# Eight images side by side in the partitions: 16 KB rows in place of 4 KB rows in every DMA of a normalisation kernel

## What is computed

```python
def _gn(v, G=32, eps=1e-5):                      # 32 groups of 2 channels, per image
    g = v.reshape(B, G, C // G, H, W)
    m, s = mean(g), var(g)                       # over a group of one image
    return (g - m) / sqrt(s + eps)

def _L0_conv_ref(x):                             # masked batch norm
    m = x.sum(axis=1) != 0                       # the sum over all 64 channels
    ...                                          # mean and variance per channel, over batch and mask
    inv = 1.0 / sqrt(var + EPS)
    return where(m, x * inv, x)                  # and a rule for position (0, 0)

out = x + _L0_conv_ref(_gn(x))
```

## Time and profile before

| | |
|---|---|
| median of the runs | 1295.09 us |
| span of the profiled execution | 1293.2 us |
| HBM read + written | 268.44 + 268.44 MB, 415 GB/s over the span |
| DMA packets | 135469 |
| ScalarE busy | 816.4 us (63%) |
| VectorE busy | 796.5 us (62%) |
| TensorE busy | 741.7 us (57%) |
| GpSimd busy | 535.1 us (41%) |

### The profile page before, as it was taken

The page is one execution under the profiler, slowest core; times in us unless marked ns, Lnnn a source line. Parts: engine busy times, 40 slices in busy tenths (PEclk is TensorE's granted clock), DMA queues, the critical chain, the costliest instruction groups (busy, mean ns, idle before and its releaser), DMA issues.

```text
span 1293.2 us, 10692 instructions
## 1 busy us (share of the span) xinstructions
PE 741.7 (57%) x2882; PEld 302.4 (23%) x2882; DVE 796.5 (62%) x1892; ACT 816.4 (63%) x950; POOL 535.1 (41%) x504
## 2 busy tenths in 40 slices
PE   0766654566545665456654566544665446654475
PEld 0222222222222222122221222212222122222232
DVE  6776666566665666655666556665566655666563
ACT  0777555775557755567655676556765567755575
POOL 0055333454334544345443444434443444533450
PEclk9988767887678876688766887667887678866788
DMA  9999999999999999999999999999999999999997
GB/s 378 415 421 420 421 421 421 422 420 420 421 421 421 420 421 421 421 421 420 421 421 421 421 421 420 421 420 421 421 421 421 420 420 421 418 421 418 420 414 281
DMA packets 135469, 537.58 MB, mean 416 GB/s; under 512 B 4336, under 2 KB 4336, under 8 KB 135408
## 3 DMA queue, kind: packets, MB, share of 16 engines
q1 hardware_dynamic: 69936, 276.83, 52.3%
q10 hardware_dynamic: 65472, 260.05, 49.0%
HBM read 268.44 MB, written 268.44 MB: 415 GB/s over the span
## 4 chain that ended last, share of the span: by engine, by line
DMA 60%; ACT 15%; PE 11%; DVE 7%; issue 5%; SPq 0%; ACTq 0%
DMA out_dram<-slots 37%; DMA slots<-in_x_dram 23%; ACT slots L346 11%; PE flush L421 6%; ACT fresh L343 4%; DVE stats L471 2%; DVE spread L454 2%; PE stay L417 1%; PE stay L418 1%; PE small_ps L386 1%; PE small_ps L396 1%; DVE dev L517 1%; PE small_ps L397 1%; ACT sums L343 0%; SPq L237 0%
## 5 line engine op out<-in xcount | busy, mean ns | idle before, releaser
L471 DVE BATCH_NORM_STATS2 stats<-slots 128x6 f32<-128x512 f32 x1024 | 631.5, 680 | 437.8 <-DMA slots<-in_x_dram 436.5
L346 ACT ACTIVATE slots<-slots,out_bias,out_scale 128x1024 f32<-128x1024 f32 x512 | 622.4, 1245 | 2.3 <-DVE out_bias L528 1.3
L325 POOL TENSOR_TENSOR sums<-fresh,sums 128x512 f32<-128x512 f32 x360 | 458.8, 1274 | 363.6 <-ACT fresh L343 363.6
L421 PE MATMUL flush<-slots,weights 128*64 128x512 f32 x1536 | 442.0, 695 | 42.2 <-ACT fresh L343 40.6
L343 ACT ACTIVATE fresh<-flush,group_bias 128x512 f32<-128x512 f32 x360 | 246.5, 685 | 51.8 <-PE flush L421 51.8
L302 POOL TENSOR_TENSOR weights<-pair_sum,group_rstd 128x256 f32<-128x256 f32 (+1 forms) x128 | 73.2, 602 | 357.5 <-DVE group_bias L508 357.5
L421 PEld LDWEIGHTS flush<-slots,weights 128*64 128x64 f32 x1536 | 131.7, 156 | 295.9 <-issue 294.3
L358 ACT ACTIVATE by_image<-by_image,eps 128x16 f32<-128x16 f32 x32 | 9.8, 307 | 242.2 <-DVE by_image L495 241.8
L417 PE MATMUL stay<-slots,weights 128*64 128x512 f32 x512 | 140.0, 606 | 0.0
L418 PE MATMUL stay<-minus_mean,weights 128*64 128x512 f32 x512 | 138.1, 593 | 0.0
L386 PE MATMUL small_ps<-spread,group_avg 128*128 128x64 f32 x64 | 21.8, 443 | 183.3 <-DVE spread L491 183.3
(11 more groups left out here) (52 smaller groups left out, 234.5 us busy)
## 6 DMA issues: line engine op xcount, KB each, us to landing
slots<-in_x_dram SPq DMA_DIRECT2D x127, 2048.0 KB, 17.7
out_dram<-slots ACTq DMA_DIRECT2D x124, 2048.0 KB, 29.9
out_dram<-slots SPq DMA_DIRECT2D x16, 512.0 KB, 5.1
slots<-in_x_dram SPq DMA_DIRECT2D x4, 512.0 KB, 13.6
```

Of the source, the lines that this page charges most:

```text
L325: pool.tensor_tensor(into, fresh[:, n % FRESH_BUFS, :], into, ALU.add).then_inc(added, 1)
L346: nc.scalar.activation(out_in_ring(u, i), image_in_ring(u, i), ACT.Identity, bias=out_bias[:, u % 2, i:i + 1], scale=out_scale[:, u % 2, i ...
L421: nc.tensor.matmul(into, weight, source, start=True, stop=True).then_inc(image_summed, 1)
L471: last = V.bn_stats(stats[:, u % 2, k * BLOCK_STATS:(k + 1) * BLOCK_STATS], source)
```

## The change

In place of 128 rows of 4 KB of one image, a DMA now takes 16 rows of eight images (`SIDE` = 8). The 512 KB of a unit and image are cut into 16 rows of 32 KB (`SET_N` = 8192 elements), and partition `8 r + a` holds row `r` of image `a` of a set of eight; there are `SETS` = 2 sets per unit. A tile is the first or the second 16 KB of these 128 rows: 2 MB as before, in 128 contiguous pieces of 16 KB, both in DRAM and in a partition. The outermost dimension of the DRAM side of a DMA is now the 16 rows, the next the eight images. The last tile's loads and the last unit's stores take 1024 columns at a time (`chunk_in_dram`), as before 512 KB in 4 KB pieces.

The sums follow. A chunk of 1024 columns now holds a sixteenth of eight images instead of one image; all small operands have 2 columns where they had 16, with 32 values where there were 4 (`FOLDS`). `group_avg` is no longer one value: VectorE builds it from the unit matrix with two more instructions at the start, so that only the partitions of the same image are averaged, and the tenth load and all of TensorE wait for four matrices instead of two. `weights` has one matrix per set and sign instead of one per image. Number and width of the `bn_stats`, of the large matmuls, of ScalarE's large instructions and of GpSimd's additions are the same. The diff, cut to this (what it changes of the general path is left out):

```diff
-TILE_IMAGES = 4
+SIDE = 8
+TILE_CHUNKS = 4
...
-    FOLDS = 2 * BLOCKS
+    SETS = B // SIDE
+    SET_N = SIDE * N
+    SET_TILES = SET_N // TILE_N
+    FOLDS = 2 * BLOCKS * SIDE
...
-    x_rows, out_rows = (t.rearrange("b c w h -> b (c w h)").rearrange("b (u p n) -> u p b n", u=UNITS, p=P) for t in (x, out))
+    x_rows, out_rows = (t.rearrange("b c w h -> b (c w h)").rearrange("(t a) (u r n) -> u t r a n", a=SIDE, u=UNITS, n=SET_N)
+                        for t in (x, out))
...
-        weights = sb("weights", [P, 2, B, ROWS])
+        weights = sb("weights", [P, 2, 2, SETS, ROWS])
...
-        CONSTS, MATRICES = 8, 2
+        CONSTS, MATRICES = 8, 4
...
         def in_dram(rows, j):
-            i = j % UNIT_TILES * TILE_IMAGES
-            return rows[j // UNIT_TILES, :, i:i + TILE_IMAGES, :]
+            t, part = divmod(j % UNIT_TILES, SET_TILES)
+            return rows[j // UNIT_TILES, t, :, :, part * TILE_N:(part + 1) * TILE_N]
+
+        def chunk_in_dram(rows, u, i):
+            at = i % SIDE * N
+            return rows[u, set_of(i), :, :, at:at + N]
...
-                    sp.dma_start(in_ring(j), in_dram(x_rows, j)).then_inc(loaded[j % RING], 16)
+                    sp.dma_start(tile_in_ring(j), in_dram(x_rows, j)).then_inc(loaded[j % RING], 16)
...
-            def weigh(u, first, n, matrix):
-                at = u * B + first
-                return pool.tensor_tensor(weights[:, u % 2, first:first + n, :], matrix.unsqueeze(1).to_broadcast([P, n, ROWS]),
-                                          group_rstd[:, at:at + n].unsqueeze(2).to_broadcast([P, n, ROWS]), ALU.mult)
+            def weigh(u, t, sign, matrix):
+                at = u * SETS + t
+                return pool.tensor_tensor(weights[:, u % 2, sign, t, :], matrix,
+                                          group_rstd[:, at:at + 1].to_broadcast([P, ROWS]), ALU.mult)
...
-                act.dma_start(in_dram(out_rows, j), in_ring(j)).then_inc(stored[j % RING], 16)
+                act.dma_start(in_dram(out_rows, j), tile_in_ring(j)).then_inc(stored[j % RING], 16)
...
             V.tensor_scalar(minus_pair_sum[:, :], pair_sum[:, :], -1.0, None, ALU.mult).then_inc(matrices_ready, 1)
+            V.tensor_reduce(side[:, :], unit_matrix.rearrange("p (j a) -> p a j", a=SIDE), AX_X, ALU.add).then_inc(matrices_ready, 1)
+            dve.wait_ge(matrices_ready, 3)
+            V.tensor_scalar(group_avg[:, :].rearrange("p (j a) -> p j a", a=SIDE), side[:, :].unsqueeze(1).to_broadcast([P, P // SIDE, SIDE]),
+                            1.0 / (HALF_UNIT * IMAGE_FOLDS), None, ALU.mult).then_inc(matrices_ready, 1)
```

More of the change, by code:

```diff
@@ L71, in flush_order, with set_of, set_order @@
         return [i for i in sum_order(u) if i in flushed]
-    x_rows, out_rows = (t.rearrange("b c w h -> b (c w h)").rearrange("b (u p n) -> u p b n", u=UNITS, p=P) for t in (x, out))
+    x_rows, out_rows = (t.rearrange("b c w h -> b (c w h)").rearrange("(t a) (u r n) -> u t r a n", a=SIDE, u=UNITS, n=SET_N)
+                        for t in (x, out))
+    def set_of(i):
+        return i // SIDE
+    def set_order(u):
+        return sorted(range(SETS), key=lambda t: sum_order(u).index(next(i for i in sum_order(u) if set_of(i) == t)))
     ctx = ExitStack()
@@ L110, in norm_conv_kernel @@
         eps = sb("eps", [P, 2])
+        side = sb("side", [P, SIDE])
+        all_avg = sb("all_avg", [P, P])
         group_avg = sb("group_avg", [P, P])
@@ L143, in norm_conv_kernel @@
         small_ps = psum("small_ps", [P, BLK])
-        mean_ps, var_ps = (small_ps[:, i * B * FOLDS:(i + 1) * B * FOLDS] for i in range(2))
+        mean_ps, var_ps = (small_ps[:, i * SETS * FOLDS:(i + 1) * SETS * FOLDS] for i in range(2))
         bn_mean_ps, bn_var_ps, count_ps = (small_ps[:, 128 + i:129 + i] for i in range(3))
@@ L166, in norm_conv_kernel @@
         flag_ready = sem("flag_ready")
-        last_loaded = [sem(f"last_loaded{i}") for i in range(TILE_IMAGES)]
+        last_loaded = [sem(f"last_loaded{i}") for i in range(TILE_CHUNKS)]
         last_stored = sem("last_stored")
@@ L255, in _, with set_in_dram, set_on_chip, load_half @@
                         sp.dma_start(into[:, :, k, :], not_zero[k * ROWS:(k + 1) * ROWS, :, :]).then_inc(mask_spread, 16)
[L257 to L261, removed]
+                def set_in_dram(rows, u, t):
+                    return rows[bass.ds(u, 1), t, :, :, :].rearrange("o r a n -> (o r) a n")
+                def set_on_chip(v, t):
+                    at = t % HALF_SETS * SET_N
+                    return v[:, at:at + SET_N]
+                def load_half(u, a):
+                    for t in range(a * HALF_SETS, (a + 1) * HALF_SETS):
+                        sp.dma_start(set_on_chip(tile_x, t), set_in_dram(x_rows, u, t)).then_inc(tile_loaded, 16)
                 for sweep in range(2):
@@ L369, in _ @@
                     put_out(u, i)
-                    if u < LAST and i and i % TILE_IMAGES == 0:
-                        store(u, i // TILE_IMAGES - 1)
+                    if u < LAST and i and i % TILE_CHUNKS == 0:
+                        store(u, i // TILE_CHUNKS - 1)
                 if u < LAST:
@@ L413, in channel_sums @@
                     for k in range(BLOCKS):
-                        into, weight = bank[k * ROWS:(k + 1) * ROWS, :], weights[:, u % 2, i, :]
+                        into = bank[k * ROWS:(k + 1) * ROWS, :]
+                        weight = weights[:, u % 2, 1 if u == LAST and i in flushed else 0, t, :]
                         source = image_in_ring(u, i)[:, k * BLK:(k + 1) * BLK]
@@ L595, in tile_g @@
                 def tile_g(sweep, u, a, k):
-                    dve.wait_ge(tile_loaded, u * (HALVES * 16) + (sweep * GENERAL_TILES + a + 1) * 16)
-                    for i in range(HALF_IMAGES):
-                        at = bass.ds(u * B + (a * HALF_IMAGES + i), 1)
-                        last = V.tensor_scalar(tile_a[:, i * N:(i + 1) * N], tile_x[:, i * N:(i + 1) * N], group_mean[:, at],
+                    dve.wait_ge(tile_loaded, u * (HALVES * HALF_MOVES) + (sweep * GENERAL_TILES + a + 1) * HALF_MOVES)
+                    for i in range(HALF_SETS):
+                        at = bass.ds(u * SETS + (a * HALF_SETS + i), 1)
+                        columns = slice(i * SET_N, (i + 1) * SET_N)
+                        last = V.tensor_scalar(tile_a[:, columns], tile_x[:, columns], group_mean[:, at],
                                                group_rstd[:, at], ALU.subtract, ALU.mult)
```

144 lines of the change are left out of this document (80 added, 64 removed).

## The result

The changed kernel takes 1460.3 us (median of four runs, 1446.9 to 1469.9) where the kernel before takes 1295.1. The run of 1469.9 us counts as a slow one, and the ratio of the other three to the kernel before is 1.124, with an interval of 1.118 to 1.130. The forecast was 1270, so the sign was wrong; rival A is what happened, at a little over half of its price (165 us for 287). The runs of the changed kernel spread over 23 us, where those of the kernel before lie within 0.4 us; no run looked for the reason of this spread.

The account below looks back on a forecast made before the run. The DMA engines were taken to bound the kernel up to the last load's landing. Terms of -24.4, -0.2 and -0.3 us (-24.9) took 1295.1 to 1270.2 us; the range was 1255 to 1610, rivals included.

Parts of the forecast that it names:

- rival A: DMA engines moving eight neighbouring partitions each share a way into on-chip memory: 1.25 x DMA time, 1582 us, chance 0.38.
- What bounds the kernel: Up to the last load's landing at 1250.06 us, time is bytes over DMA rate; behind it DMA engines aren't full.
- Part 1: Loads and stores in 16 KB instead of 4 KB pieces: 1.95% less time up to the last landing, 24.4 us.
- The prediction's own sign for it: Sign of a wrong forecast: two directions cost more with 16 KB packets than with 4 KB ones.
- Its sign at the start: For shared ways on chip: tiles landing every 6 us or more already at the start, with loads alone.
- Parts 2 to 4: Small operands with fewer columns (0.2 us gained), fewer GpSimd weight instructions (0.3 us), two more instructions at the start (nothing).
- The end: Statistics, ScalarE's work and the rest behind the last load's landing: still 43 us after the change.
- Rivals B and C: B: images 16.8 MB apart slow DRAM, 1670 us, chance 0.06. C: packet time is all bytes, 1294.6 us, chance 0.10.

Follow-up runs that it names:

- streams: Kernel of DMAs only, thirty tiles loaded and thirty others stored, neither waiting for the other; all in 16 KB pieces: 337.6 us with eight images, 295.5 with four.

## Why the prediction was wrong

**What bounds the kernel: right.** The DMA engines are full before and after. Two readings were loose: the rate has fallen to 369 GB/s already at 1255 to 1262, and of the 43 us behind the last load, where the DMA engines were said not to be full, the stretch from 1270 to 1280 has a share of 1.02 at 403 GB/s.

**Part 1, its size: right where the split is right.** A unit went from 40.2 to 39.4 us with four images, for the forecast 39.5. Loads alone and mixed are both at 430 GB/s with 16 KB pieces, for 410 and 421 in the kernel before and 402 and 419 with four images in 4 KB pieces. At the same split a 16 KB packet saves 2.3% of a unit (40.28 to 39.37), and 2.6% of the rate in streams (431 against 420 GB/s). The forecast 1.95% was near, but partly by luck: it is three quarters of the gap between loads alone and loads with stores. That gap is gone with 16 KB pieces, but no run shows that it is what a packet costs as such.

**The step that failed: part 1, worked out as if the split over the DMA engines stayed the same.** Part 1 was to take 24.4 us off the time up to the last load's landing. That time went up by 157.3 us, from 1250.06 to 1407.35. Part 1 priced only the packets and put the change of which DMA engine moves which partitions at nothing. The diff changes it: the outermost dimension of the DRAM side went from 128 to 16. With the pieces at 16 KB, rows of eight partitions in place of four take loads alone from 430 to 216 GB/s and a unit from 39.37 to 43.55 us. The prediction's own sign for it came out too: a unit costs more with 16 KB packets than with 4 KB ones (43.55 and 40.57 us), once the split is bad.

The weighing went wrong with it. I gave rival A 0.38 and the forecast 0.46, with the reason that "for it speaks only the shape". The shape is what decides. The trace of the kernel before couldn't speak, since with its split the rate is 410 GB/s or more from the start. For a case without a row the two rules of the Trainium skill that rival A names were all there was, they agreed with each other and with the diff, and they should have weighed more.

**Rival A: the mechanism right, the size not.** 1582 forecast, 1460 measured. Its sign at the start was right (tiles every 9.7 us, "6 us or more"). Its 25% in the mixed stretch is 10.6% against the good split. It assumed that partners meet at random in both directions and whatever the packet's length; in fact loads alone stay in step (216 GB/s), stores alone mostly fall out of it (428 GB/s after 30 us), and in the mixed stretch the loss is only 0.7% with 4 KB packets. The range to 1610 held the time.

**A step that was missing: the last tile.** I counted its four DMAs as unchanged, "as before 512 KB in 4 KB pieces". They were, but the stores in the other queue weren't. This costs the last unit 14 us in the changed kernel.

**Parts 2 to 4: right as far as the rows show.** The instructions with 2 columns take 161 ns where those with 16 took 175 (L543 of the changed kernel; L506). GpSimd's are 293 ns. The two new ones end at 3.19 us, ten before the first tile. What parts 2 and 3 gain in the last unit, 0.5 us, is too small to be seen beside the rest.

**The end: 5 us off.** I forecast 43 us behind the last load; it is 37.7 (1445.0 - 1407.35), a term that I had taken as fixed. From 1407 to 1417 the DMA engines are idle (share 0.01), where the kernel before still moved 369 GB/s at 1255 to 1262: the last tile is so late that all older stores are done. That this is what shortens the end was not tested.

**Rivals B and C** fall with the four images: 430 GB/s with neighbours 16.8 MB apart, and not 421. Eight images side by side have no loss either where no two rows collide (216 GB/s with half of the DMA engines at partitions 32 to 95). The Trainium skill's rule on rows 4 MiB or more apart (DMA: Bandwidth & Descriptors, "Latency and other measured facts") doesn't show in these two runs, where images 16.8 MB apart alternate within a DMA.

**What stays open.** That 4 KB pieces lose nothing in a mixed stretch while loads alone lose 40% is less odd than it looks: at 420 GB/s with equal bytes each way the loads need 210, and loads alone reach 216 to 241 with the same split. If one partner loads while the other stores, neither waits. This reading is argued from the rates and was not tested. Why 4 KB packets come to that alternation almost fully (420 GB/s) and 16 KB packets only to 379 to 398 is open, and so is why loads alone in 4 KB pieces ran at 241 GB/s at the start of the kernel and at 304 to 306 in the streams, after the stores had ended. Which DMA engines lag behind at the end was not looked at either.

## What to carry to other kernels

When the access pattern of a DMA changes, ask first what its outermost dimension is on both sides and which partitions each DMA engine gets; loads alone in rows of four neighbouring partitions ran at 430 GB/s and the same bytes in rows of eight at 216. Larger pieces are worth some 2.3% from 4 to 16 KB in a kernel that is all DMA. If one queue's pieces get larger, look for urgent small pieces in the other queue.

## What the runs showed of the hardware

Loads alone in rows of eight partitions stay near half the rate for as long as they were watched, 100 us (210 to 216 GB/s on one queue, 224 to 228 on two), though one stage with 8 rows ran at 127 GB/s where half would be 108. Stores alone start there and are at 428 GB/s after 30 us on one queue, but on two queues only at 380 to 390. The DMA share is 0.96 to 1.01 at 215 GB/s and 1.01 at 428, so a full DMA engine doesn't say that bytes move: only GB/s does. Beside 16 KB packets in the other queue, 512 KB in 4 KB pieces take 6.1 us. The Trainium skill (DMA: Bandwidth & Descriptors, "Queues, rings and completion order") has the turn by packet, and the trace agrees: 8 turns of a 16 KB and a 4 KB packet are 8 x (0.61 + 0.16) = 6.2 us.
